# Block-diagonal attention and MLP on one core: heads in row tiles of 64, paired PSUM banks, and one order for each engine

## What is computed

```python
x = L0_attn_x                                    # (32, 512, 256)
qkv = layernorm(x) @ w_qkv.T + b_qkv             # 16 heads of 16
scores = einsum('bhqd,bhkd->bhqk', q * scale, k) + mask
out = einsum('bhqk,bhkd->bhqd', softmax(scores), v)
x = x + layernorm(out @ w_out.T + b_out)
x = x + layernorm(relu(layernorm(x) @ W1 + b1) @ W2 + b2)   # 256 -> 1024 -> 256
```

## Time and profile before

| | us |
|---|---|
| median of 3 runs | 2374.32 (2372.41 to 2374.86) |
| span of the profiled execution | 2371.9 |
| PE busy | 2296.9 (97%) |
| PE weight loads busy | 1917.6 (81%) |
| DVE busy | 1739.7 (73%) |
| ACT busy | 1487.9 (63%) |
| POOL busy | 781.8 (33%) |

### The profile page before, as it was taken

The page is one execution under the profiler, slowest core; times in us unless marked ns, Lnnn a source line. Parts: engine busy times, 40 slices in busy tenths (PEclk is TensorE's granted clock), DMA queues, the critical chain, the costliest instruction groups (busy, mean ns, idle before and its releaser), DMA issues.

```text
span 2371.9 us, 59261 instructions
## 1 busy us (share of the span) xinstructions
PE 2296.9 (97%) x18176; PEld 1917.6 (81%) x18176; DVE 1739.7 (73%) x3909; ACT 1487.9 (63%) x3077; POOL 781.8 (33%) x1159
## 2 busy tenths in 40 slices
PE   5899999999999999999999999999999999999997
PEld 3678888888888888888888888888888888888876
DVE  5777777777777777777777777777777777777742
ACT  3456666666666666666666666666666666666654
POOL 0023332333332333332333332333332333332344
PEclk8989999999999999999999999999999999999998
DMA  6444444344444444444344444444444444444410
GB/s 141 95 85 80 87 87 93 78 88 78 86 86 93 78 88 78 86 85 92 79 88 78 86 85 92 79 88 79 86 85 92 79 88 79 86 85 84 82 33 18
DMA packets 158659, 197.93 MB, mean 83 GB/s; under 512 B 37392, under 2 KB 88336, under 8 KB 158600
## 3 DMA queue, kind: packets, MB, share of 16 engines
q1 hardware_dynamic: 107400, 146.83, 34.4%
q10 hardware_dynamic: 51200, 50.34, 6.7%
HBM read 37.25 MB, written 16.78 MB: 23 GB/s over the span
## 4 chain that ended last, share of the span: by engine, by line
PE 88%; DVE 5%; DMA 3%; issue 2%; ACT 1%; POOL 1%; SPq 0%; DVEq 0%; POOLq 0%; ACTq 0%
PE p_lin L425 29%; PE p_lin L490 15%; PE p_max L359 8%; PE p_o L408 7%; PE p_sc L383 7%; PE p_max L354 6%; PE p_o L405 5%; PE p_sc L378 5%; PE p_lin L417 3%; DMA stack<-max_row 2%; PE p_lin L453 2%; DVE neg_max L646 2%; PE p_lin L438 1%; DVE max_row L677 1%; POOL h_lo L789 1%
## 5 line engine op out<-in xcount | busy, mean ns | idle before, releaser
L533 ACT ACTIVATE probs<-p_sc 128x512 f32<-128x512 f32 x1280 | 725.3, 603 | 590.4 <-PE p_sc L378 317.2
L646 DVE TENSOR_REDUCE neg_max<-p_max 128x2 f32<-128x512 f32 (+1 forms) x1280 | 856.0, 679 | 192.3 <-PE p_max L359 112.7
L789 POOL TENSOR_TENSOR h_lo<-h_f,h_hi 128x256 fp32r<-128x256 f32 x512 | 364.9, 732 | 512.1 <-ACT h_hi L571 505.9
L359 PE MATMUL p_max<-stack 72*128 72x256 f32 x1536 | 341.6, 304 | 19.5 <-DVE neg_max L646 19.2
L571 ACT ACTIVATE h_f<-p_lin,b_s 128x256 f32<-128x256 f32 x512 | 243.4, 475 | 120.7 <-PE p_lin L425 120.3
L359 PEld LDWEIGHTS p_max<-stack 72*128 72x128 f32 x1536 | 244.0, 191 | 89.6 <-issue 52.2
L383 PE MATMUL p_sc<-stack 80*128 80x256 f32 x1536 | 310.2, 284 | 0.0
L425 PE MATMUL p_lin<-x_hi,w_hi 128*128 128x256 f32 (+1 forms) x1280 | 297.3, 314 | 3.7 <-ACT h_hi L571 2.0
L490 PE MATMUL p_lin<-w_hi,h_hi 128*128 128x256 f32 x1024 | 292.6, 286 | 7.2 <-POOL h_lo L789 6.0
L383 PEld LDWEIGHTS p_sc<-stack 80*128 80x128 f32 x1536 | 273.8, 192 | 28.9 <-ACT probs L533 0.7
L490 PE MATMUL p_lin<-w_lo,h_hi 128*128 128x256 f32 x1024 | 291.2, 284 | 0.0
(11 more groups left out here) (81 smaller groups left out, 3767.2 us busy)
## 6 DMA issues: line engine op xcount, KB each, us to landing
stack<-qk SPq DMA_DIRECT2D x2048, 64.0 KB, 2.3
xa<-x ACTq DMA_DIRECT2D x32, 512.0 KB, 3.9
xr<-x ACTq DMA_DIRECT2D x32, 512.0 KB, 3.5
out<-yf ACTq DMA_DIRECT2D x64, 256.0 KB, 2.5
stack<-max_row SPq DMA_DIRECT2D x256, 32.0 KB
probs<-w SPq DMA_DIRECT2D x2, 512.0 KB, 4.7
probs<-w_qkv_t SPq DMA_DIRECT2D x2, 384.0 KB, 5.0
x_old<-w SPq DMA_DIRECT2D x1, 512.0 KB, 6.9
```

The costliest lines, as they stand in the source:

```text
L359: last = nc.tensor.matmul(dst[:, j * 2 * P:(j + 1) * 2 * P].rearrange("p (a n) -> p a n", a=2), q_stack[0:MAXROW, buf, j, kb * P:(kb + 1) ...
L533: nc.scalar.activation(probs[:, CH * (p % 2) + c, :], p_sc[k % 2][:, :], ACT.Exp, scale=SCALE).then_inc(exp_done, 1)
L646: nc.vector.tensor_reduce(dst, src, axis=AX.X, op=ALU.max, negate=True).then_inc(red_done, 1)
L789: last = nc.gpsimd.tensor_tensor(h_parts[1][:, m, :], h_f[:, n % 2, u, :], h_parts[0][:, m, :].bitcast(F32), ALU.subtract)
```

## The change

The way in which scores are packed and the order are rewritten; the arithmetic of the layers is kept.

- **Row tiles.** The contraction falls from 72 and 80 rows to 48 and 49: q and k in three parts and, in the second pass, one row of maxima against a row of ones. The two heads of a pair lie in `stack` at partitions 0 to 48 and 64 to 112, and every step issues each matmul twice (`for j in range(2)`), once for either head, from its own rows into its own bank.
- **Quads and bank pairs.** A step covers two banks (`p_att[j]`, 128 x 2 x 512). Three such pairs form one ring for both passes: the n-th step of PE's list takes pair n mod 3, and waits until the step that had it before was reduced or exponentiated. A quad of heads has five steps in a pass: c = 0 and 1 are block 0 against all for one pair of heads each, two matmuls of 512 columns; c = 2 to 4 are four matmuls of 256 columns. DVE reduces the 1024 columns of a step with one instruction and ACT takes their exp with one.
- **Maxima.** For a quad four transposes of 128 x 4 ("max_t"), one copy of 4 x 512 and two transfers of two rows, in place of two transposes, two masked multiplications and two transfers. The mask constants go.
- **Linears.** Two banks in turn instead of three, and "pv" (probabilities times values) is one of the units: one block of 32 matmuls for a quad, where before it came in two halves with score steps between them.
- **In place.** The second layer norm writes over `xr`, where it wrote `xh`; before that ACT has to copy `xr` (`x1_keep` waits for x1_done, `ln2_apply` for x1_kept). Loads of x and the stores move from ACT's queue to SP's.
- **Order.** Each engine has its own list, ORDER, of (job, number, item offset). The loop runs turns 5 to 11 of these lists, with offsets of up to 20 for SP; the other turns are written out. In PE's list a turn has 40 score steps and 38 units, and 35 changes between three kinds of work: score steps (row tiles of 64), pv (column tiles of 32) and the rest (the full array). 4 of the 35 lead into pv.

```diff
-    STACK = 4 * HD
-    MAXROW = STACK + 2 * KB
-    K_ALL = MAXROW + 2 * KB
+    VW = HD + 1
+    ROW = P // 2
+    STACK = 3 * HD
+    K_ALL = STACK + 1
-    LIN = 3
+    ATT, LIN = 3, 2
-        p_max = [ps(f"p_max{j}", [P, L]) for j in range(2)]
-        p_sc = [ps(f"p_sc{j}", [P, L]) for j in range(2)]
+        p_att = [ps(f"p_att{j}", [P, 2, L]) for j in range(ATT)]
         p_lin = [ps(f"p_lin{j}", [P, L]) for j in range(LIN)]
-        p_o = ps("p_o", [P, L])
+        def step_parts(c):
+            if c < 2:
+                return [(c, 0, 0)]
+            if c < 4:
+                return [(c - 2, 1, 0), (c - 2, 2, HALF)]
+            return [(0, 3, 0), (1, 3, HALF)]
+            def scores(dst, quad, c, stationary, moving, rows):
+                for m, (pair, kb, col) in enumerate(step_parts(c)):
+                    at = 2 * quad + pair
+                    for j in range(2):
+                        r = slice(ROW * j, ROW * j + rows)
+                        if kb == 0:
+                            last = nc.tensor.matmul(dst[:, j, :], stack[r, stationary, at, 0:P],
+                                                    stack[r, moving, at, :], start=True, stop=True)
+                        else:
+                            last = nc.tensor.matmul(
+                                dst[:, j, col:col + HALF].rearrange("p (a n) -> p a n", a=2),
+                                stack[r, stationary, at, kb * P:(kb + 1) * P],
+                                two(stack[r, moving, at, :], kb), start=True, stop=True)
+                return last
+            def job(what, n, b, i):
+                before = unit_before(what, n, i)
+                if before:
+                    wait(pe, free[before[0]], before[2], COUNT[before[0]], before[1] + 1)
+ORDER = {
+    "PE": [
...
+        ("pv", 3, -1), ("v", 0, 0), ("v", 1, 0), ("x1", 0, 1), ("scores", 0, 0), ("scores_max", 9, 0),
+        ("scores", 1, 0), ("o_t", 3, -1), ("x1", 1, 1), ("scores", 2, 0), ("o2", 1, -1), ("qk", 0, 1),
...
+    "SP": [
...
+        ("load_row", 0, 18), ("load_stack", 5, 18), ("store", 0, 16), ("load_stack", 6, 18), ("load_xa", 0, 20),
+        ("load_xr", 0, 17), ("load_row", 1, 18), ("load_stack", 7, 18),
```

More of the change, by code:

```diff
@@ L216, in there, with first @@
             return not isinstance(b, int) or 0 <= b < NB
-        def above(b, k):
-            return not isinstance(b, int) or b > 0 or k > 0
+        def first(b, n):
+            return isinstance(b, int) and b == 0 and n == 0
         def wait(eng, s, b, per, k):
@@ L228, in wait, with bank @@
                 eng.wait_ge(s, b * per + k)
-        def place(what, which):
-            return [job[:2] for job in UNITS].index((what, which))
-        def bank_of(at):
-            return at % len(UNITS) % LIN
+        free = {"scores_max": red_done, "scores": exp_done, "pv": ot_done, **ev}
+        def bank(what, which):
+            units, banks = (STEPS, p_att) if what in ("scores_max", "scores") else (UNITS, p_lin)
+            return banks[[job[:2] for job in units].index((what, which)) % len(banks)]
@@ L244, in unit_before, with steps, turn @@
                     return name, n, b
             return None
-        def bank(what, which):
-            return p_lin[bank_of(place(what, which))]
-        def steps(eng, step, setup):
+        def steps(eng, jobs, job, early=None):
+            def turn(i):
+                todo = [(what, n, i + off) for what, n, off in jobs if there(i + off)]
+                for at, (what, n, b) in enumerate(todo):
+                    if early and not isinstance(i, int):
+                        early(what, todo[at + 1:])
+                    job(what, n, b, i)
@@ L545, in job @@
[L545 to L552 removed]
+            act.dma_start(xa[:, :, :], x_t[0]).then_inc(xa_in, 16)
@@ L558, in job @@
                         for p in range(4 * (n // 2), 4 * (n // 2) + 4):
[L559 to L561 removed]
+                            wait(act, stack_in[p], b, 96, 0)
+                    nc.scalar.activation(qk[:, n // 2, 2 * (n % 2), :], bank("qk", n)[:, :], ACT.Identity,
                                          bias=bqk_s[:, n:n + 1]).then_inc(hi_done["qk"], 1)
[L563 removed]
+                    if n == 1 and isinstance(b, int) and b == 0:
+                        split_rest()
+                elif what == "relu":
                     half = n // 4
@@ L765, in _, with statistics_done @@
+            def statistics_done(what, following):
+                for next_what, n, b in () if what.endswith("_mean") else following:
+                    if not next_what.endswith("_mean"):
+                        break
+                    wait(dve, bn_done[next_what[:3]], b, 2, n + 1)
+            steps(dve, ORDER["DVE"], job, statistics_done)
         @block.gpsimd
```

723 lines of the change are left out of this document (326 added, 397 removed), and 27 rows, old and new, of the table SCHEDULE.

## The result

| | before | after |
|---|---|---|
| median of the runs, us | 2374.59 (4 runs, 2372.41 to 2375.70) | 2273.05 (4 runs, 2267.57 to 2274.08) |
| ratio, 95% interval | | 0.957 (0.956 to 0.959) |
| span of the profiled execution, us | 2371.9 | 2265.8 |
| PE busy, us | 2296.9 (97%) | 2116.1 (93%) |
| DVE / ACT busy, us | 1739.7 / 1487.9 | 1567.3 / 1418.0 |

The changed kernel is 4.3% faster. I had predicted 2307 us (2.8% faster) with a range of 2150 to 2415. It takes 34 us less than predicted.

What follows compares the result with a forecast made beforehand. PE was taken to set the pace: its work of 65.7 us plus 3.3 of waits gave 69.0 a turn; 32 turns plus 96.4 made a span of 2304.4, and 2.4 more the forecast of 2307 us, range 2150 to 2415.

Steps and rivals of the forecast that it cites:

- the rival on the clock: PE's idle time lowers its granted clock to a mean of 0.95, some 3.3 us a turn: 2413 us; chance 0.04.
- Row tiles (9.6 us): Score matmuls on PE run side by side in twos, 160 units become 80: 9.6 us a turn, 9.6 saved.
- weight loads in a row: Loads of the two row tiles share one path, a 256-column pair takes 0.216 us: 73.6 a turn, 2454 us; chance 0.12.
- no overlap: Paired score matmuls in row tiles do not run side by side: 9.6 us a turn more, 2610 us; chance 0.02.
- Changes (6.6 us): PE's 35 changes of kind a turn: 31 at 0.20 us, 4 into pv at 0.10; 6.6 against 2.4 before.
- cheap changes: Full array and row tiles hand over without the 0.20 us: a turn of 64.4 us, 2160 us; chance 0.13.
- Products (34.6 us): PE's 288 units of 256-column products a turn, at 0.12 us each, stay at 34.6 us as before.
- Waits (3.3 us): PE waiting for late ACT and DVE answers, 3.3 us a turn against 0.9 before; above 5 would prove it wrong.
- the step that costed SP's transfers at nothing: Maxima rows are needed about 4 us or more after their copy, a transfer lands in 2.3: no cost.
- The rival of doubled waits: Late DVE answers delay those behind them, 3.3 us more a turn: 72.3, 2413 us; chance 0.09.
- DVE and ACT: 1024-column reduction 1.20 us, exp 1.02; DVE down to about 50 us a turn, ACT to about 43; neither the bound.
- Filling and emptying: Filling and emptying the pipeline, outside the 32 turns, kept at 96.4 us; bounds 75 to 105.

Runs made afterwards that it cites:

- experiment 1: Changed kernel with both heads of each score step read from partitions 0 to 48, so a pair shares one row tile (scores wrong); 2496.43 us, 1.052 of before.
- Experiments 2 and 3: 2: changed kernel, score matmuls reading 65 rows (full array), 2399.90 us. 3: kernel before, first-pass score matmuls reading 64 rows instead of 72, 2791.01 us.
- experiment 9: Changed kernel with o2, x2 and h put back at the addresses of the kernel before; 2300.99 us, 0.969 of before.
- Experiment 6: Changed kernel with each reduction and each exp of 1024 columns made as two of 512, one for each bank; 2279.49 us, 0.959 of before.
- experiment 2: Changed kernel with every score matmul reading 65 rows, so it takes the full array (scores wrong); 2399.90 us, 1.011 of before.
- experiment 4: Changed kernel with ln2_apply 1 ahead of qk_lo 3 on DVE and x1_keep 1 ahead of qk_hi 3 on ACT; 2274.21 us, 0.958 of before.

## Why the prediction held, and where it didn't

- **PE bounds, a turn is the unit, clock.** Right. The granted clock was 1.00 from 170 to 2140 us although PE idles more; the rival on the clock is out.
- **Row tiles (9.6 us).** Right, 9.3: full overlap, loads included. The rivals "weight loads in a row" (pairs 0.216 us apart) and "no overlap" are out; experiment 1 gives the price of the latter, 6.9 us a turn and not 9.6, because waits vanish in it.
- **Changes (6.6 us).** Right, 6.2. The step took 0.20 for each of 31 from the way out of p_o; changes into row tiles and into products cost 0.19, those into transposes 0.15 (0.09, and 0.165 instead of 0.109 for the first transpose). Experiments 2 and 3 show it from both sides, so "cheap changes" is out.
- **Products (34.6 us).** Wrong, 33.4. The step took the 34.6 "as before". It is the mis-sized term: 1.2 us a turn, 38 us in all, more than the whole miss. Two things are in it. A unit was rounded up to 0.12 us, where the pitches of the kernel before add up to 34.2 us: 0.4 us a turn. The other 0.8 to 0.9 us, some 27 us in all, came with the tiles that had moved, and experiment 9, which moves them back, costs 28. The instructions were the same. The first could be read from the trace of before, the second could not.
- **Waits (3.3 us).** The places were right but for one, and the size was too small: 4.4. qk behind the transposes of xa 0.6 (predicted 0.55), the f1 run 0.5 (0.4) and the maxima behind it 0.6 (0.5), the second layer norm 0.7 and 0.1 (0.6 and 0.2), the bank of the projection 0.3 (0.32), the maxima and f1 behind a late x_lo 0.24 and 0.3 (0.2 each). Not foreseen were 0.1 more on the first product behind two of these waits, 0.15 within a run of score steps, 0.1 in front of the second transposes of xa, and 0.24 on average in front of the o_t behind the third qk product. The last one is the wait of ACT for the transfers into `stack`, so the step that costed SP's transfers at nothing was too low by that much. The rival of doubled waits (6.6) is out; 4.4 is a third of the way to it, and below the 5 that the prediction had named as the sign.
- **DVE and ACT.** 1.21 and 1.03 us as estimated, by the page 1567.3/32 = 49.0 us a turn for DVE (about 50) and 1418.0/32 = 44.3 for ACT (about 43). Experiment 6 shows that the saving from paired banks is worth 0 to 12 us of the time.
- **Filling and emptying.** 96.4 was taken as before; it is about 90, within the bounds given.
- **The sum.** 32 x (69.0 - 68.0) is 32 us, filling 6 more: a span 38 us below the one predicted. The runs' median lies 7 us above the profiled span and not 2.4, which leaves the 34. That products too high by 1.2 and waits too low by 1.1 nearly met was luck; the other terms, each too high by 0.1 to 0.4, made the rest.

No version that I ran is measurably faster than the changed kernel. What remains uncounted is the new order by itself: no run gives the kernel before the new order, or the changed one the old.

## What to carry to other kernels

Contractions of up to 64 rows can be worth pairing in row tiles, here even at 31 changes of mode a turn (3.9 us a turn by experiment 2), if each visit holds enough work: a change costs 0.15 to 0.19 us, as much as a pair and a half of 256 columns, and a pair saves 0.12. When the bounding engine's own work shrinks, some of it comes back as waits that it had covered: a quarter and two fifths in the two cases here (9.2 to 6.9 us, 5.0 to 2.9). When two steps of another engine stand ahead of a wait, swapping them gives nothing (experiment 4); taking work off that engine may, but no run here tried it. Before crediting a rewrite with its last per cent, compare the pitch of instructions that it did not touch: here tiles that moved in SBUF gave 18 to 28 of the 101 us.

## What the hardware showed that I had not expected

- The pitch of a 256-column fp32r product depends on where its operands lie. In f2, with the tiles 64 bytes apart modulo 128, a row of products locks into one of two values to 0.1 ns: 113.3 or 117.8. With the tiles 0 apart it lies between 118.2 and 120.2. A row at 117.8 has single starts 117 to 119 ns apart, so it is no mixture of 113 and 120.
- Which of the two values a row takes is not a matter of the addresses alone. From 400 to 2000 us some nine tenths of f2's products follow at 113.3 in the changed kernel, eight tenths in experiment 1 and a quarter in experiment 2, all with the same tiles at the same addresses. What picks it stays open.
- Pairs in two row tiles mostly start 3 to 4 ns apart, and their weight loads, 128 columns each, don't delay each other: the next pair starts 0.117 to 0.122 us later.
- 65 rows count as the full array, 64 rows as a row tile, and the way out of either into the other costs 0.09 us, as much as the way into column tiles.
